# A new order of work on TensorE, with the other engines' queues rearranged to match, in a kernel of two small transformers around a retention layer

## The chip, the cores and the metric

One core of one Trainium2 chip runs the whole program. The metric is the device time of one execution in microseconds (us), median of three runs. TensorE (PE, with its weight loads PEld), VectorE (DVE), ScalarE (ACT) and GpSimd (POOL) each work through a queue of their own in the order in which it is written; semaphores are all that ties them together.

## The reference, cut to what matters

```python
for i in range(6):                                    # DEPTH; x is (1, 2048, 128), run twice: before and after
    x = attn_layer(shift_tokens(x), ...) + x          # a retention layer
    x = ffn_layer(shift_tokens(x), ...) + x
# attn_layer: 16 heads of 64, window 32
q, k, v = x @ Wqkv
q, k = l2norm(q) * qs, l2norm(k) * ksc                # then rotated by tables
sim = q @ k_of_two_windows * 8;  attn = softmax(masked sim);  out = (attn @ v) @ Wo
# ffn_layer
xn = layernorm(x) * g + b;  a, gate = (xn @ W1 + b1);  out = a * gelu(gate) @ W2 + b2
```

All of it is float32. The kernel folds Wv and Wo of a layer into one matrix per head (V'), so that attention's last product, P times V', is summed over the heads in PSUM and gives the layer's output at once.

## The kernel before

The tokens are cut into 16 tiles of 128 per layer, 96 tiles per stack of six layers, and there are two stacks (`stack(0)`, the retention layer, `stack(1)`). A stack is a software pipeline of slots: in slot c each engine runs its part `slot(c, None, s)` with tile n = c at stage 0, tile n-1 at stage 1 and so on to stage 5. The functions are:

- Stage 0: `project_qk(0..3)`, four 128x512 projections of q and k into the two banks of QA, on PE (L838). ACT squares each (`square`, L451), DVE rotates it (`rotate`, L603 and L608) and sums the squares (`square_sum`, L616), POOL adds the two halves of the rotation (`rot_add`, L343). A projection into a bank waits until the projection two before has been rotated. The inverse norm is worked out as NRM (DVE L677), LT and RN (ACT L541, L543), LA and RR (DVE `inverse_norm`, L621, L624, L629); POOL multiplies it in (`norm_mult`, L350).
- Stage 1 and 2: `qk_transpose` (PE L926), four pieces 0 to 3 of four transpositions each, copied to QT and KT by ACT (`qk_out`, L465); `mask_scores` and `scores` (PE L936, L952). The maximum MX and the difference Z are DVE's (L687, L691).
- Stage 3: ACT's exponential of Z (L512), DVE's sums SM and reciprocal RC (L667, L671), POOL's `softmax_mult` (L359). `p_transpose(3, 0)` and, one slot later, `p_transpose(4, 1)` transpose P (PE L881), ACT copies it to PT (`p_out`, L477).
- Stage 4: `project_v(0..3)`, V' in four pieces, 128x32 tiles of the array side by side (PE L902), copied by ACT (`v_out`, L471). Pieces 0 and 1 wait for Z of the previous slot, since they use the banks of the scores; pieces 2 and 3 wait for the copies of 0 and 1.
- Stage 5: `attend`, P times V', 64 matmul instructions of 128x32 (PE L857); ACT copies the result ON (L499); `out_transpose` (PE L865); DVE's `attn_residual` (L635) adds it to Y. In the kernel before DVE does this last part near the end of the slot ahead of PE's `out_transpose`, so it waits there for PE's next slot.

TB has two banks: bank 0 holds P's transpositions and pieces 0 and 3 of q and k, bank 1 holds `attend`, `out_transpose` and pieces 1 and 2. So `qk_transpose(1, 1)` waits for the residual (`s_res`) of tile n-5.

The feed-forward part runs for groups of four tiles. Slots therefore come in fours: the centre slot (c % 4 = 0: `ffn_centre` L965, `ffn_variance` L970, in stack 0 also `fold_weights` L1005), the up0 slot (`ffn_up(.., 0)`, L980 and L981), the up1 slot and the up2 slot (`ffn_up(.., 2)` right behind `project_qk(0)`, and three `ffn_down`, L989). In the last three ACT runs a Gelu (L485) with one table load ahead of it and one behind; DVE's `hidden` (HB, L642) needs it.

PE's order of a slot before, with the feed-forward parts left out, is: `project_qk(0)`, `attend`, `p_transpose(4, 1)`, `project_v(0, 1)`, `out_transpose`, `project_qk(1)`, `qk_transpose(1, 0)` and `(1, 1)`, `project_v(2, 3)`, `project_qk(2, 3)`, `qk_transpose(2, 3)`, `mask_scores`, `qk_transpose(1, 2)`, `scores`, `p_transpose(3, 0)`.

Of the kernel before, what the change touches and what calls it, by code (L numbers as in the profile page):

```python
# [54 lines left out]
def build_macaron(nc, x, w_qk, w_vt, w_out, q_rows, w1, w2, prm_ffn, w_ret, gn, tables, consts, mask_n, ident,  # L55
# [5 lines left out]
    with ctx:  # L61
# [52 lines left out]
        LNB = sb("LNB", [P, 1])  # L114
        RST = sb("RST", [P, 24])
# [204 lines left out]
        def _(po):  # L320
# [5 lines left out]
            po.memset(LNB[:, :], 8.0 * 0.6931471805599453).then_inc(s_cst, 1)  # L326

            def slot(c, it, s):
# [44 lines left out]
                if live(c, 1, it):  # L373
                    norm_mult(1, 1)
                if live(c, 0, it):
                    rot_add(0)
                if live(c, 1, it):
                    norm_mult(1, 2)
                if live(c, 0, it):
                    rot_add(1)  # L380
                if live(c, 3, it):
                    softmax_mult()
                if live(c, 2, it) and (c - 2) % 4 == 3:
                    last_keys()
                if live(c, 0, it):
                    rot_add(2)
                if live(c, 1, it):
                    norm_mult(1, 3)
# [54 lines left out]
        def _(ac):  # L443
            def slot(c, it, s):
# [46 lines left out]
                if up0_g is not None:  # L491
                    ac.wait_ge(s_var, by_group(1, s * GROUPS + up0_g, it, 1))
                    nc.scalar.activation(RS[:, :], FB[:, 1, :], ACT.Ln, bias=EPS[:, 0:1]).then_inc(s_fl, 1)
                    ac.wait_ge(s_fl, by_group(1, s * GROUPS + up0_g, it, 1))
                    nc.scalar.activation(RS[:, :], RS[:, :], ACT.Exp, scale=-0.5).then_inc(s_frs, 1)
                if live(c, 5, it):
                    m = n - 5
                    ac.wait_ge(s_o, by_tile(1, m, it, 1))
                    nc.scalar.activation(ON[:, m % 2, :], TB[:, 1, 0:P], ACT.Copy).then_inc(s_oe, 1)  # L499
                if live(c, 4, it):  # L500
                    p_out(4, 1)
                    v_out(0)
                if live(c, 0, it):
                    square(0)
                if live(c, 4, it):
                    v_out(1)
                if live(c, 0, it):
                    square(1)
                if live(c, 3, it):
                    m = n - 3  # L510
                    ac.wait_ge(s_z, by_tile(1, m, it, 1))
                    nc.scalar.activation(Z[:, m % 2, :], Z[:, m % 2, :], ACT.Exp, scale=8.0).then_inc(s_ex, 1)  # L512
                if live(c, 1, it):
                    qk_out(1, 0)
                    qk_out(1, 1)
                if live(c, 4, it):
                    v_out(2)
                if live(c, 0, it):
                    square(2)
                if live(c, 4, it):  # L520
                    v_out(3)
                if live(c, 0, it):
                    square(3)
# [13 lines left out]
                if live(c, 3, it):  # L537
                    p_out(3, 0)
                if live(c, 0, it):
                    ac.wait_ge(s_rm, by_tile(1, n, it, 1))  # L540
                    nc.scalar.activation(LT[:, n % 2, :], NRM[:, n % 2, :], ACT.Ln, scale=LN_SCALE).then_inc(s_rl, 1)  # L541
                    ac.wait_ge(s_rl, by_tile(1, n, it, 1))
                    nc.scalar.activation(RN[:, n % 2, :], LT[:, n % 2, :], ACT.Exp, scale=-0.5, bias=LNB[:, 0:1])\  # L543
                        .then_inc(s_re, 1)
                if (c - 7) % TPL == 0 and (it is not None or c < TILES):
# [10 lines left out]
            ac.wait_ge(s_cst, 5)  # L556
# [34 lines left out]
        def _(ve):  # L591
            def slot(c, it, s):
# [39 lines left out]
                def attn_residual(rows, one):  # L632
                    m = n - 4
                    a = (m % TPL) * P + one
                    return nc.vector.tensor_tensor(Y2[rows, a:a + P], TB[rows, 1, 0:P], Y[rows, a:a + P], ALU.add)  # L635
# [12 lines left out]
                if live(c, 0, it):  # L648
                    rotate(0)
                    rotate(1)  # L650
                if fold_piece(c, s):
# [8 lines left out]
                if live(c, 0, it):  # L660
                    square_sum(0)
                    square_sum(1)
                if live(c, 3, it):
                    m = n - 3
                    ve.wait_ge(s_ex, by_tile(1, m, it, 1))
                    for e in range(2):
                        nc.vector.tensor_reduce(SM[:, m % 2, e, :], Z[:, m % 2, e * GT:(e + 1) * GT].rearrange(  # L667
                            "p (a c k) -> p c a k", a=2, c=CH), AX.XY, ALU.add).then_inc(s_sum, 1)
                    ve.wait_ge(s_sum, by_tile(2, m, it, 2))
                    need(ve, s_pn, by_tile(2, m - 1, it))  # L670
                    nc.vector.reciprocal(RC[:, m % 2, :, :], SM[:, m % 2, :, :]).then_inc(s_rc, 1)  # L671
                if live(c, 0, it):
# [23 lines left out]
                if live(c, 0, it):  # L696
                    inverse_norm()
# [21 lines left out]
                if live(c, 4, it):  # L719
# [21 lines left out]
            ve.wait_ge(s_cst, 5)  # L741
# [81 lines left out]
        def _(pe):  # L823
            mm = nc.tensor.matmul

            def slot(c, it, s):
# [195 lines left out]
                if up2_g is not None:  # L1022
                    ffn_up(up2_g, 2)
                if live(c, 5, it):
# [9 lines left out]
                if live(c, 0, it):  # L1034
                    project_qk(1)
                if live(c, 1, it):
                    qk_transpose(1, 0)
                    qk_transpose(1, 1)
                if live(c, 4, it):
                    project_v(2)  # L1040
                    project_v(3)
                if live(c, 0, it):
# [208 lines left out]
```

## Time and profile before

| | |
|---|---|
| median of 3 runs | 3528.91 us (3528.77 to 3534.39) |
| the profiled execution, its time / its span | 3533.1 us / 3531.3 us |
| busy share PE, DVE, ACT, POOL | 96%, 81%, 67%, 66% |
| mean granted TensorE clock | 0.984 |
| four slots in the middle of stack 1 | 66.58 us, PE busy throughout |

The profile shows one execution. A row of the timeline is a run of instructions of one line: its start in us from the span's start, its length, and in brackets how long the engine was idle before and what ended that. Matmuls are pipelined and a matmul's length includes its drain, so what a block costs on PE is the distance from its start to the next block's start.

### The profile page before, as it was taken

The page shows a single profiled execution, that of the slowest core. Times are in us where ns is not written, and L with a number is a line of the kernel's source. Part 1 is how long each engine was busy: PE and PEld are TensorE (multiplying, and loading weights), DVE is VectorE, ACT ScalarE, POOL GpSimd, SP SyncE. Part 2 cuts the span into 40 slices and gives each one's busy share as a digit, 9 for nine tenths or more (in the row PEclk, how much of TensorE's full clock was granted, in tenths as well). Part 3 has the DMA queues.
Part 4 walks back from the last instruction along what each step waited for, and adds up shares of the span by engine and source line. Part 5 has one row for each costly group of instructions (what it writes and reads, how often), then busy time and mean ns, then how long its engine had stood idle before and what let it go on. Part 6 is the DMA issues. An engine that isn't in the chain of part 4 may idle for free.

```text
span 3531.3 us, 123143 instructions
## 1 busy us (share of the span) xinstructions
PE 3402.0 (96%) x51660; PEld 1851.7 (52%) x51660; DVE 2847.4 (81%) x6052; ACT 2365.6 (67%) x4133; POOL 2333.9 (66%) x2187
## 2 busy tenths in 40 slices
PE   6999999999999999999788999999999999999996
PEld 3555555555555555555354555555555555555553
DVE  6888888888888888886468888888888888888883
ACT  3676677667677667767424777677767767767764
POOL 5766667676677677775137777677677677667761
PEclk8999999999999999999998999999999999999998
DMA  2001001001001001000100000000000000000000
GB/s 83 11 14 47 12 14 47 13 15 47 12 14 47 13 14 35 9 12 20 38 2 23 14 23 22 17 23 22 12 29 22 12 27 23 12 27 10 12 5 13
DMA packets 49223, 76.64 MB, mean 22 GB/s; under 512 B 7072, under 2 KB 37024, under 8 KB 47136
## 3 DMA queue, kind: packets, MB, share of 16 engines
q1 hardware_dynamic: 48672, 68.76, 6.1%
q8 instruction: 411, 6.73, 0.8%
q14 instruction: 140, 1.15, 0.1%
HBM read 61.39 MB, written 7.34 MB: 19 GB/s over the span
## 4 chain that ended last, share of the span: by engine, by line
PE 93%; DVE 3%; issue 2%; POOL 1%; ACT 1%; DMA 0%; SPq 0%; DVEq 0%; POOLq 0%; ACTq 0%
PE VS L902 20%; PE QA L838 19%; PE TB L857 10%; PE TB L926 9%; PE VS L952 8%; PE TB L881 6%; PE FB L980 4%; PE FB L989 4%; PE FB L981 4%; PE VS L936 2%; PE TB L865 1%; PE FB L965 1%; PE FB L970 1%; DVE T L608 1%; POOL QN L343 0%
## 5 line engine op out<-in xcount | busy, mean ns | idle before, releaser
L343 POOL TENSOR_TENSOR QN<-T 128x512 f32<-128x512 f32 x768 | 979.9, 1276 | 578.6 <-DVE T L608 578.6
L350 POOL TENSOR_TENSOR QN<-QN,RR 128x512 f32<-128x512 f32 x768 | 800.7, 1043 | 296.9 <-DVE RR L629 296.9
L838 PE MATMUL QA<-WQ,Y 128*128 128x512 f32 x1536 | 797.8, 618 | 20.2 <-DVE T L608 12.1
L902 PE MATMUL VS<-MW,Y 128*32 128x512 f32 x6144 | 741.8, 600 | 5.0 <-DVE Z L691 5.0
L451 ACT ACTIVATE SQ<-QA 128x512 f32<-128x512 f32 x768 | 458.8, 597 | 294.0 <-PE QA L838 268.7
L608 DVE TENSOR_TENSOR T<-QA,TAB 128x256 f32<-128x256 f32 x1536 | 570.7, 412 | 0.0
L603 DVE TENSOR_TENSOR T<-QA,TAB 128x512 f32<-128x512 f32 x768 | 513.6, 669 | 38.1 <-ACT SQ L451 23.2
L471 ACT ACTIVATE V<-VS 128x512 f32<-128x512 f32 x768 | 461.0, 600 | 95.1 <-PE VS L902 94.5
L926 PEld LDWEIGHTS TB<-CST,QN 128*128 128x128 f32 x3072 | 374.2, 142 | 256.8 <-issue 191.6
L359 POOL TENSOR_TENSOR Z<-Z,RC 128x512 f32<-128x512 f32 x384 | 394.5, 1048 | 142.8 <-DVE RC L671 142.8
L616 DVE TENSOR_REDUCE SSQ<-SQ 128x8 f32<-128x512 f32 x768 | 487.2, 676 | 0.0
L635 DVE TENSOR_TENSOR Y<-TB,Y 64x128 f32<-64x128 f32 x384 | 111.2, 290 | 464.6 <-PE TB L865 461.9
L926 PE MATMUL TB<-CST,QN 128*128 128x128 f32 x3072 | 437.9, 275 | 15.0 <-POOL QN L350 14.3
L838 PEld LDWEIGHTS QA<-WQ,Y 128*128 128x128 f32 x1536 | 263.1, 199 | 309.5 <-DVE T L608 176.3
L857 PEld LDWEIGHTS TB<-V,PT 128*32 128x32 f32 x12288 | 325.9, 110 | 153.1 <-issue 111.8
L857 PE MATMUL TB<-V,PT 128*32 128x128 f32 x12288 | 381.5, 274 | 4.4 <-issue 4.3
L477 ACT ACTIVATE PT<-TB 128x512 f32<-128x512 f32 x384 | 228.9, 596 | 196.5 <-PE TB L881 196.2
L902 PEld LDWEIGHTS VS<-MW,Y 128*32 128x32 f32 x6144 | 161.0, 109 | 300.3 <-issue 295.0
L952 PEld LDWEIGHTS VS<-KT,QT 64*32 64x32 f32 x24576 | 255.7, 105 | 105.0 <-issue 88.2
L465 ACT ACTIVATE KT<-TB 128x512 f32<-128x512 f32 x384 | 231.6, 603 | 116.2 <-PE TB L926 116.2
L952 PE MATMUL VS<-KT,QT 64*32 64x64 f32 x24576 | 290.8, 225 | 16.0 <-issue 15.9
L687 DVE TENSOR_REDUCE MX<-VS 128x8 f32<-128x512 f32 x384 | 245.4, 679 | 29.9 <-PE VS L952 25.7
(166 smaller groups left out, 4206.0 us busy)
## 6 DMA issues: line engine op xcount, KB each, us to landing
TAB<-in_tables SPq DMA_DIRECT2D x192, 128.0 KB, 2.1
WQ<-in_w_qk SPq DMA_DIRECT2D x48, 256.0 KB, 2.9
m_dram<-MW SPq DMA_DIRECT2D x6, 1024.0 KB, 5.4
MW<-m_dram SPq DMA_DIRECT2D x6, 1024.0 KB, 5.2
W1R<-in_w SPq DMA_DIRECT2D x12, 341.0 KB, 3.0
WS<-in_w_vt SPq DMA_DIRECT2D x6, 512.0 KB, 5.9
WS<-in_w_out SPq DMA_DIRECT2D x6, 512.0 KB, 7.8
W<-in_w SPq DMA_DIRECT2D x12, 192.0 KB, 2.4
```

Source lines behind the costliest of these rows:

```text
L343: po.tensor_tensor(QN[:, n % 2, k, :], T1[:, k, :], T2[:, k, :], ALU.add).then_inc(s_add, 1)
L350: po.tensor_tensor(heads(QN[:, m % 2, k, :]), heads(QN[:, m % 2, k, :]), RR[:, m % 2, 8 * k:8 * k + 8].unsqueeze(2).to_broadcast([P, 8, DH ...
L451: nc.scalar.activation(SQ[:, k % 2, :], QA[:, k % 2, :], ACT.Square).then_inc(s_sq, 1)
L471: nc.scalar.activation(V4[:, m % 4, w, :], VS[:, w % 2, :], ACT.Copy).then_inc(s_ve, 1)
L603: nc.vector.tensor_tensor(heads(T1[:, k, :]), heads(QA[:, b, :]), tab[:, 0:DHEAD].unsqueeze(1).to_broadcast([P, 8, DHEAD]), ALU.mult)
L608: ins = nc.vector.tensor_tensor(t2[:, :, half, :], q2[:, :, 1 - half, :], tab[:, DHEAD + 32 * half:DHEAD + 32 * half + 32].unsqueeze(1).to ...
L616: nc.vector.tensor_reduce(SSQ[:, n % 2, 8 * k:8 * k + 8], heads(SQ[:, k % 2, :]), AX.X, ALU.add)\
L838: mm(QA[:, k % 2, :], Y[:, j * P:(j + 1) * P], WQ[:, k, :], start=True, stop=True).then_inc(s_qk, 1)
L857: last = mm(TB[32 * w:32 * w + 32, 1, 0:P], PT[:, m % 2, b, 32 * w:32 * w + 32], v, start=(b == 0), stop=(b == CH - 1), tile_position=(0, ...
L902: last = mm(VS[32 * q:32 * q + 32, w % 2, :], Y[:, a:a + WIN], MW[:, l % 2, q, :], start=True, stop=True, tile_position=(0, 32 * q), skip_ ...
L926: last = nc.tensor.transpose(TB[:, (0, 1, 1, 0)[k], b * P:(b + 1) * P], QN[:, m % 2, k, b * P:(b + 1) * P], IDF)
L952: last = mm(bank[32 * w:32 * w + 32, :, ch, :], QT[r, m % 2, ch, w * WIN:(w + 1) * WIN], KT[r, ch, a:a + 2 * WIN].rearrange("p (a k) -> p ...
```

## The change

The order within a slot is rewritten on four engines; the instructions stay the same but one. PE: `project_qk(1)` moves up behind `project_qk(0)`, `p_transpose(4, 1)` stands ahead of `attend`, `attend` stands directly ahead of `project_v(0, 1)`, and the three blocks `qk_transpose(1, 0)`, `out_transpose`, `qk_transpose(1, 1)` stand in different places: the first two behind `project_v(0, 1)`, the last behind `project_v(2, 3)`. DVE: `attn_residual` now handles tile n-5 behind the first two square sums, the fold copy is later, `inverse_norm` stands ahead of MX and Z instead of behind them, and NRM is a TENSOR_TENSOR maximum with a constant tile TINY instead of a TENSOR_SCALAR. ACT: squares 0 and 1, `p_out(4, 1)` and the exponential come first, LT and RN stand ahead of `p_out(3, 0)`. POOL: `norm_mult(1, 2)` and `(1, 3)` come one and two places earlier.

```diff
 PE
                 if live(c, 0, it):
                     project_qk(0)
                 if up2_g is not None:
                     ffn_up(up2_g, 2)
+                if live(c, 0, it):
+                    project_qk(1)
+                if live(c, 4, it):
+                    p_transpose(4, 1)
                 if live(c, 5, it):
                     attend()
                 if live(c, 4, it):
-                    p_transpose(4, 1)
                     project_v(0)
                     project_v(1)
+                if live(c, 1, it):
+                    qk_transpose(1, 0)
                 if live(c, 5, it):
                     out_transpose()
                 if fold_piece(c, s):
                     fold_weights(*fold_piece(c, s))
-                if live(c, 0, it):
-                    project_qk(1)
-                if live(c, 1, it):
-                    qk_transpose(1, 0)
-                    qk_transpose(1, 1)
                 if live(c, 4, it):
                     project_v(2)
                     project_v(3)
+                if live(c, 1, it):
+                    qk_transpose(1, 1)
                 if live(c, 0, it):
                     project_qk(2)
 DVE
                 if live(c, 0, it):
                     rotate(0)
                     rotate(1)
+                    square_sum(0)
+                    square_sum(1)
+                if live(c, 5, it):
+                    ve.wait_ge(s_ot, by_tile(1, n - 5, it, 1))
+                    attn_residual(*HALVES[0])
+                    attn_residual(*HALVES[1]).then_inc(s_res, 1)
...
-                    nc.vector.tensor_scalar_max(NRM[:, n % 2, :], SSQ[:, n % 2, :], 1e-24).then_inc(s_rm, 1)
+                    nc.vector.tensor_tensor(NRM[:, n % 2, :], SSQ[:, n % 2, :], TINY[:, :], ALU.max).then_inc(s_rm, 1)
                 if up1_g is not None:
                     hidden(up1_g, 1)
                 if live(c, 0, it):
                     rotate(3)
+                    inverse_norm()
                 if live(c, 2, it):
...
-                if live(c, 0, it):
-                    inverse_norm()
...
-                if live(c, 4, it):
-                    ve.wait_ge(s_ot, by_tile(1, n - 4, it, 1))
-                    attn_residual(*HALVES[0])
-                    attn_residual(*HALVES[1]).then_inc(s_res, 1)
                 if up0_g is not None:
                     hidden(up0_g, 0)
 ACT, new order
+                square(0), square(1), p_out(4, 1), exponential(3), ON copy(5), v_out(0), v_out(1), qk_out(1, 0),
+                v_out(2), v_out(3), qk_out(1, 1), square(2), square(3), qk_out(2, 3)
...
                 if live(c, 1, it):
                     qk_out(1, 2)
-                if live(c, 3, it):
-                    p_out(3, 0)
                 if live(c, 0, it):
                     (LT, RN)
+                if live(c, 3, it):
+                    p_out(3, 0)
```

## Rows read from the trace of the kernel before

**Rows 1.** The page, busy time and share of the span.
```profile
PE 3402.0 (96%) x51660; PEld 1851.7 (52%) x51660; DVE 2847.4 (81%) x6052; ACT 2365.6 (67%) x4133; POOL 2333.9 (66%) x2187
```

**Rows 2.** Windows: four slots of stack 1; length, busy times, granted clock.
```profile
2899.40:2966.00 66.60, 66.60 (x1061) 36.09 (x1060) 56.72 (x124) 47.96 (x84) 47.78 (x45) 1.00 0.03 10
```

**Rows 3.** Timeline of PE, the up1 slot from 2931.41 us on.
```profile
2931.41 1.02 PE L838 MATMUL QA<-WQ,Y 128*128 128x512 f32 x2
2932.36 1.95 PE L857 MATMUL TB<-V,PT 128*32 128x128 f32 x64
2934.24 0.66 PE L881 MATMUL TB<-CST,Z 128*128 128x128 f32 x4
2934.83 1.92 PE L902 MATMUL VS<-MW,Y 128*32 128x512 f32 x16
2936.68 0.33 PE L865 MATMUL TB<-CST,ON 128*128 128x128 f32 x1
2936.85 1.02 PE L838 MATMUL QA<-WQ,Y 128*128 128x512 f32 x2
2937.71 1.04 PE L926 MATMUL TB<-CST,QN 128*128 128x128 f32 x8
2938.68 1.92 PE L902 MATMUL VS<-MW,Y 128*32 128x512 f32 x16
2940.53 1.98 PE L838 MATMUL QA<-WQ,Y 128*128 128x512 f32 x4
2942.35 0.60 PE L926 MATMUL TB<-CST,QN 128*128 128x128 f32 x4
...
2947.43 1.02 PE L838 MATMUL QA<-WQ,Y 128*128 128x512 f32 x2
```

**Rows 4.** Groups by line: busy us, mean ns of one, idle before.
```profile
L857 PEld LDWEIGHTS TB<-V,PT 128*32 128x32 f32 x12288 | 325.9, 110 | 153.1 <-issue 111.8
...
L704 DVE SCALAR_TENSOR_TENSOR Y<-FB,PRB,Y 64x512 f32<-64x512 f32 x96 | 71.8, 748 | 13.1 <-PE FB L989 12.4
```

**Rows 5.** Timeline of DVE, end of the up0 slot and the up1 slot.
```profile
2931.02 1.29 DVE L687 TENSOR_REDUCE MX<-VS 128x8 f32<-128x512 f32 x2
...
2933.42 0.18 DVE L621 TENSOR_TENSOR LA<-RN 128x32 f32<-128x32 f32 x1
...
2933.86 0.19 DVE L629 SCALAR_TENSOR_TENSOR RR<-LA,RN 128x32 f32<-128x32 f32 x1
2937.05 0.59 DVE L635 TENSOR_TENSOR Y<-TB,Y 64x128 f32<-64x128 f32 x2 [2.99 <-PE TB L865]
2937.67 0.75 DVE L642 SCALAR_TENSOR_TENSOR HB<-FB,PRB,GE 128x512 f32<-128x512 f32 x1
2938.34 0.68 DVE L603 TENSOR_TENSOR T<-QA,TAB 128x512 f32<-128x512 f32 x1
...
2940.86 1.27 DVE L616 TENSOR_REDUCE SSQ<-SQ 128x8 f32<-128x512 f32 x2
2942.05 1.27 DVE L667 TENSOR_REDUCE SM<-Z 128x8 f32<-128x512 f32 x2
```

**Rows 6.** Timeline of ACT, end of the up0 slot and the up1 slot.
```profile
2929.60 0.69 ACT L485 ACTIVATE GE<-FB,PRB 128x512 f32<-128x512 f32 x1 [0.57 <-PE FB L981]
2930.31 1.28 ACT L531 ACT_TABLE_LOAD   x1
2931.61 0.60 ACT L465 ACTIVATE QT<-TB 128x512 f32<-128x512 f32 x1
2932.10 0.59 ACT L477 ACTIVATE PT<-TB 128x512 f32<-128x512 f32 x1
2932.58 0.23 ACT L541 ACTIVATE LT<-NRM 128x32 f32<-128x32 f32 x1
2932.84 0.32 ACT L543 ACTIVATE RN<-LT,LNB 128x32 f32<-128x32 f32 x1
...
2938.41 1.05 ACT L512 ACTIVATE Z<-Z 128x1024 f32<-128x1024 f32 x1
```

More of the change, by code:

```diff
@@ L114, in build_macaron @@
         LNB = sb("LNB", [P, 1])
+        TINY = sb("TINY", [P, 32])
         RST = sb("RST", [P, 24])
@@ L326, in _ @@
             po.memset(LNB[:, :], 8.0 * 0.6931471805599453).then_inc(s_cst, 1)
+            po.memset(TINY[:, :], 1e-24).then_inc(s_cst, 1)
             def slot(c, it, s):
@@ L374, in slot @@
                     norm_mult(1, 1)
+                    norm_mult(1, 2)
                 if live(c, 0, it):
@@ L377, in slot @@
                 if live(c, 1, it):
-                    norm_mult(1, 2)
+                    norm_mult(1, 3)
                 if live(c, 0, it):
@@ L495, in slot @@
                     nc.scalar.activation(RS[:, :], RS[:, :], ACT.Exp, scale=-0.5).then_inc(s_frs, 1)
+                if live(c, 0, it):
+                    square(0)
+                    square(1)
+                if live(c, 4, it):
+                    p_out(4, 1)
+                if live(c, 3, it):
+                    m = n - 3
+                    ac.wait_ge(s_z, by_tile(1, m, it, 1))
+                    nc.scalar.activation(Z[:, m % 2, :], Z[:, m % 2, :], ACT.Exp, scale=8.0).then_inc(s_ex, 1)
                 if live(c, 5, it):
@@ L500, in slot @@
                 if live(c, 4, it):
-                    p_out(4, 1)
                     v_out(0)
-                if live(c, 0, it):
-                    square(0)
-                if live(c, 4, it):
                     v_out(1)
-                if live(c, 0, it):
-                    square(1)
-                if live(c, 3, it):
-                    m = n - 3
-                    ac.wait_ge(s_z, by_tile(1, m, it, 1))
-                    nc.scalar.activation(Z[:, m % 2, :], Z[:, m % 2, :], ACT.Exp, scale=8.0).then_inc(s_ex, 1)
                 if live(c, 1, it):
                     qk_out(1, 0)
-                    qk_out(1, 1)
                 if live(c, 4, it):
                     v_out(2)
+                    v_out(3)
+                if live(c, 1, it):
+                    qk_out(1, 1)
                 if live(c, 0, it):
                     square(2)
-                if live(c, 4, it):
-                    v_out(3)
-                if live(c, 0, it):
                     square(3)
@@ L544, in slot @@
                         .then_inc(s_re, 1)
+                if live(c, 3, it):
+                    p_out(3, 0)
                 if (c - 7) % TPL == 0 and (it is not None or c < TILES):
@@ L650, in slot @@
                     rotate(1)
+                    square_sum(0)
[4 more added lines that the diff above has]
+                    attn_residual(*HALVES[1]).then_inc(s_res, 1)
+                if live(c, 3, it):
+                    m = n - 3
+                    ve.wait_ge(s_ex, by_tile(1, m, it, 1))
+                    for e in range(2):
+                        nc.vector.tensor_reduce(SM[:, m % 2, e, :], Z[:, m % 2, e * GT:(e + 1) * GT].rearrange(
+                            "p (a c k) -> p c a k", a=2, c=CH), AX.XY, ALU.add).then_inc(s_sum, 1)
+                    ve.wait_ge(s_sum, by_tile(2, m, it, 2))
+                    need(ve, s_pn, by_tile(2, m - 1, it))
+                    nc.vector.reciprocal(RC[:, m % 2, :, :], SM[:, m % 2, :, :]).then_inc(s_rc, 1)
                 if fold_piece(c, s):
@@ L660, in slot @@
                 if live(c, 0, it):
[L661 to L672, printed above, removed]
                     rotate(2)
@@ L739, in pads @@
                 nc.vector.memset(Y2[64:128, 0:1], 0.0)
-            ve.wait_ge(s_cst, 5)
+            ve.wait_ge(s_cst, 6)
             pads()
@@ L1023, in slot @@
                     ffn_up(up2_g, 2)
+                if live(c, 0, it):
+                    project_qk(1)
+                if live(c, 4, it):
+                    p_transpose(4, 1)
                 if live(c, 5, it):
@@ L1041, in slot @@
                     project_v(3)
+                if live(c, 1, it):
+                    qk_transpose(1, 1)
                 if live(c, 0, it):
```

12 lines of the change are left out of this document (3 added, 9 removed).

## The prediction

> **What bounds the kernel now.** The page comes first: PE is busy 96% of the span, DVE 81%, ACT and POOL two thirds [rows 1]. Then the windows, to see whether that share means the same in the steady part: over four slots of stack 1 PE is busy 66.60 of 66.60 us at the full clock, while DVE has 10 us to spare and ACT and POOL 19 each [rows 2]. So nobody keeps PE waiting there, and a slot is as long as the sum of PE's blocks. The timeline of PE tells what a block costs, as the distance between starts [rows 3]; DVE's and ACT's timelines tell how late their parts of a slot are [rows 5, 6]. The reader should note DVE's wait of 2.99 us ahead of the residual: DVE, which must do the residual for the slot to come, stands still until PE has got to `out_transpose` [rows 5]. It does no harm today, because PE asks for what lies behind it later still.
>
> **What PE's order costs.** Within one kind of work the price is flat. A projection is 0.86 (2936.85 to 2937.71). A transposition is 0.11: eight of them and a change to the 128x32 form take 0.97, four and such a change 0.59. Changes of form cost extra [rows 3]:
> - full to 128x32: 0.95 from the projection to `attend`, less 0.86, is 0.09;
> - 128x32 back to full: a pair of V' pieces takes 1.85 where four times 0.43 is 1.72, so 0.13 (this holds a little for the first group of the block too);
> - the first full instruction behind it is slow as well: a lone transposition takes 0.17 instead of 0.11, so 0.06; two projections there take 1.82 instead of 1.72, so 0.10.
>
> Before, a slot has four excursions into tiled forms: `attend`, the two pairs of V', the scores. After, `attend` and the first pair are one. That saves 0.09 + 0.13 + 0.06 = 0.28. Behind the second pair there now stands a transposition in place of a projection: 0.10 becomes 0.06, a saving of 0.04 to 0.05. Splitting `qk_transpose(1, 0)` from `(1, 1)` costs nothing more, since each borders on an excursion that is there anyway. Sum 0.33 a slot. About 188 of the 192 tiles have all these neighbours (the first and last slots of a stack do not), so 188 x 0.33 = 62 us.
>
> Here the join itself was never run: the trace has no 128x32 block behind another. If its weight loads did not hide, 0.13 would stay; if they hide as inside `attend`, nothing does. Inside `attend` 12288 loads of 110 ns, 1352 us laid end to end, take 325.9 us of busy time, so four are under way at once, all of them on 128 rows, while the matmuls run on [rows 4]. I take nothing for the join and keep 0.13 x 188 = 24 us as the other bound.
> The Trainium skill speaks against the change here: "TensorE: Matmul & The Clock Gate", section "Part 3: Packing small matmuls", says that a weight load overlaps with matmuls in flight only when its row group differs, and all of these share theirs. By that rule the join would be exposed and the saving 0.20 a slot, 38 us, by my rows' prices. The L857 row does not look like it.
>
> **What must now be on time.** New starts on PE, counted from `project_qk(0)`, in a slot without feed-forward work ahead: `project_qk(1)` 0.86, `p_transpose(4, 1)` 1.72, `attend` 2.25 (four transpositions 0.44, change 0.09), `project_v(0)` 4.00 (1.88 less the 0.13 of the change back), `qk_transpose(1, 0)` 5.85, `out_transpose` 6.34, `project_v(2)` 6.55, `qk_transpose(1, 1)` 8.40, `project_qk(2)` 8.89. All distances are those of [rows 3].
>
> The weak point is DVE's new order. `inverse_norm` now stands ahead of MX and Z and waits for RN. In an up0 or up1 slot RN is late, because on ACT it stands behind the Gelu, a table load and the QT copy. The up0 slot's chain, from the start of its Gelu, is:
> - ACT: Gelu to table load 0.71, table load 1.30, QT 0.49 to the next, LT 0.26, RN 0.32: 3.08 [rows 6];
> - DVE: from LA to RR 0.44, and 0.11 to the next: 0.55; MX and Z 2.40; `hidden` 0.67; two rotations 2.52; two square sums 1.19; the residual 0.59: 7.92 [rows 5];
> - two hand-overs between engines at 0.04 each, as `out_transpose` ends at 2937.01 and the residual starts at 2937.05 [rows 3, 5]: 0.08.
>
> That is 11.08 us, and only then may `qk_transpose(1, 1)` of the up1 slot write TB's second bank, which the residual reads. The Gelu starts 1.81 before the slot's end (2929.60 against 2931.41), and nothing ahead of it changes. So the transposition can start 9.27 into the up1 slot, and PE is there at 8.40: a stall of 0.87. Behind it on PE are `project_qk(2)`, `(3)` and the rest of the slot, all of which slip. Two smaller waits fall inside it: `p_out(3, 0)`, now behind RN, ends at 1.9 where PE asks at 1.72, and Z ends at 4.3 where `project_v(0)` asks at 4.00 plus the first slip.
> It happens wherever the slot after an up0 slot has a live tile, 22 times a stack: 44 x 0.87 = 38 us.
>
> In the up2 slot PE has 1.72 more ahead of the same transposition and the residual is on time (10.2 against 10.3). But ACT has two table loads and the third Gelu ahead of squares, `p_out(4, 1)`, exponential, ON and V copies. From the Gelu of the up1 slot: 3.08 to RN's end; p_out 0.61, load 1.30, Gelu 0.70, load 1.30, then square, square, p_out at 0.49 each, exponential 0.95 (1.05 long, 0.1 overlapped as in its neighbours), ON 0.19, V 0.60: 10.2 [rows 6]. Less 1.81, V' piece 0 is copied at 8.4, and `project_v(2)`, which overwrites that bank, is due at 6.55 + 1.72 = 8.27. Stall 0.15, some 46 times: 7 us.
>
> The other slots stay free. Centre slot: in the up2 slot before it no table load stands ahead of RN, Z ends 2.3 into it, then come the two halves of Y's write at 0.7 [rows 4], two rotations, two square sums and the residual as above, done at 8.0 against 8.40; up0 slot: DVE starts at 2.5 and waits for `out_transpose`, residual done at 7.3. `project_qk(1)`, now early, needs rotation 3 of the slot before, which ends a microsecond or more ahead of the slot's end, or, where `hidden` pushes it past the end, has the up2 block of 1.72 in front. NRM as TENSOR_TENSOR saves DVE some tenths, in time in which it then waits for RN: nothing. POOL's moves are hidden: its inputs come from DVE, and it has 19 us in 66.6 free [rows 2]. TINY is one memset at the start. No DMA moves. The fold copy in stack 0 (centre slot) has the 0.8 us that PE spends on folding as cover.
>
> **Sum.** -62 + 38 + 7 = -17 us against the profiled execution's 3533.1 us, which is 3516. That execution lay 4.2 above the median, so the median should be 3512.
>
> **Rivals.**
> - *PE keeps all it saves.* The chain would have to be 0.9 us shorter, so that no new wait is seen: 3528.9 - 62 = 3467. DVE's 10 free us in 66.6 and the 2.99 us wait that goes away speak for it [rows 2, 5]; the order `RN, then MX and Z` against it, which moves the free time to a worse place. Chance 0.07.
> - *The join is exposed.* 0.13 stays in every slot: 3512 + 24, less what the shorter saving takes off the waits (PE arrives 0.13 later, so 90 times up to 0.13, some 12): 3524, within 0.2% of before. Together with other ways to come out level: chance 0.14. The skill's rule above would give this; the L857 row is against it.
> - *Slower: ACT in the up2 slot.* The copies behind its last table load are priced at 0.49 from start to start [rows 6]. If, in the new neighbourhood, each waits for its predecessor's 0.60, the seven of them on that chain add 0.8: 46 x 0.8 = 37 us, and the median would be 3549. Net zero is reached at 0.37 per up2 slot. Against it: QT to PT 0.49 in the same place. With other waits of this size that I do not see (a chain over three engines has many edges), chance 0.15.
>
> **How the numbers follow.** The forecast, a part of the saving kept, has 0.64; it runs from 3495 (stall 0.5 instead of 0.87) to 3522. A measurement of this kernel tells 0.2%, 7 us, from no change. Faster: 0.64 + 0.07, with a little of the forecast's upper end given to level: 0.69. Same 0.15, slower 0.16. The range is 3490 to 3534: it leaves out the full saving (0.07) and most of the slower case (0.13).
>
> **What would show it.** In the after profile: slots of four 66.58 - 4 x 0.33 + 1.0 = 66.2 us. `attend` to `project_v(0)` 1.77 apart; V' pair to `qk_transpose(1, 0)` 1.83 to 1.85. In up1 slots PE idle ahead of the L926 block behind the second V' pair, released by DVE's residual, some 0.9; in up2 slots a gap ahead of `project_v(2)`, released by ACT's V copy. On DVE an idle of 2.4 us ahead of LA in up0 slots, released by ACT's RN, and none of 2.99 ahead of the residual. The prediction is wrong if LA does not wait in up0 slots, if the join costs, or if another wait on PE shows in centre or up0 slots.

## The result, and the profile after

The changed kernel takes 3483.5 us (median of 4 runs, 3483.0 to 3490.1), the kernel before 3529.9 beside it: ratio 0.9871, 95% interval 0.9853 to 0.9888, 46 us faster. The forecast was 3512 with a range from 3490 to 3534; the direction was right and the size far too small. The profiled execution has a span of 3481.8 us, 49.5 less than before.

The page after, busy time of the engines and the groups with the pauses (busy us, mean ns | idle before, releaser), first of the kernel after:

```profile
PE 3337.9 (96%) x51660; PEld 1871.0 (54%) x51660; DVE 2858.4 (82%) x6052; ACT 2433.7 (70%) x4133; POOL 2342.3 (67%) x2188
...
L854 PE MATMUL TB<-V,PT 128*32 128x128 f32 x12288 | 375.2, 274 | 0.0
...
L949 PE MATMUL VS<-KT,QT 64*32 64x64 f32 x24576 | 289.0, 225 | 8.5 <-issue 8.1
```

and the same two groups of the kernel before, `attend` (L857) and `scores` (L952), as the page has them:

```profile
L857 PE MATMUL TB<-V,PT 128*32 128x128 f32 x12288 | 381.5, 274 | 4.4 <-issue 4.3
...
L952 PE MATMUL VS<-KT,QT 64*32 64x64 f32 x24576 | 290.8, 225 | 16.0 <-issue 15.9
```

PE is still 96% busy, of a shorter span: 64 us of its own busy time have gone, with the same 51660 matmul instructions. An idle "issue" is one for which the page names no releaser; it has gone inside `attend` and halved inside `scores`. No term of the forecast had that.

The timeline of PE after, up1 slot from 2425.80 us on, the counterpart of [rows 3] (L835 projections, L878 P's transpositions, L854 `attend`, L899 V', L862 `out_transpose`, L923 transpositions of q and k):

```profile
2425.80 1.88 PE L835 MATMUL QA<-WQ,Y 128*128 128x512 f32 x4
2427.70 0.63 PE L878 MATMUL TB<-CST,Z 128*128 128x128 f32 x4
2428.26 1.96 PE L854 MATMUL TB<-V,PT 128*32 128x128 f32 x64
2430.20 1.92 PE L899 MATMUL VS<-MW,Y 128*32 128x512 f32 x16
2432.06 0.66 PE L923 MATMUL TB<-CST,QN 128*128 128x128 f32 x4
2432.55 0.27 PE L862 MATMUL TB<-CST,ON 128*128 128x128 f32 x1
2432.75 1.92 PE L899 MATMUL VS<-MW,Y 128*32 128x512 f32 x16
2435.16 0.63 PE L923 MATMUL TB<-CST,QN 128*128 128x128 f32 x4 [0.48 <-DVE Y L634]
2435.62 1.88 PE L835 MATMUL QA<-WQ,Y 128*128 128x512 f32 x4
...
2442.36 0.59 PE L835 MATMUL QA<-WQ,Y 128*128 128x512 f32 x1
```

This slot is 16.56 long; before it was 16.02. The second pair of V' pieces starts at 2432.75, and the transposition behind it 2.41 later where 1.85 is the price: it waits for DVE's residual, as forecast. (The idle of 0.48 in brackets is counted from the end of the drain, so the distance of starts shows more of the loss.) The two other losses are 0.18 ahead of `p_transpose(4, 1)`, which starts 1.90 after the projections instead of 1.72, and 0.17 between `attend` and V'.

DVE and ACT of the same stretch, as in [rows 5, 6]:

```profile
2424.03 0.75 DVE L607 TENSOR_TENSOR T<-QA,TAB 128x256 f32<-128x256 f32 x2
2427.11 0.19 DVE L620 TENSOR_TENSOR LA<-RN 128x32 f32<-128x32 f32 x1 [2.32 <-ACT RN L540]
...
2427.67 1.28 DVE L690 TENSOR_REDUCE MX<-VS 128x8 f32<-128x512 f32 x2
2428.87 1.28 DVE L694 TENSOR_TENSOR Z<-VS,MX 128x512 f32<-128x512 f32 x2
2430.06 0.74 DVE L641 SCALAR_TENSOR_TENSOR HB<-FB,PRB,GE 128x512 f32<-128x512 f32 x1
2430.72 0.68 DVE L602 TENSOR_TENSOR T<-QA,TAB 128x512 f32<-128x512 f32 x1
...
2434.43 0.58 DVE L634 TENSOR_TENSOR Y<-TB,Y 64x128 f32<-64x128 f32 x2
```

```profile
2424.00 0.69 ACT L486 ACTIVATE GE<-FB,PRB 128x512 f32<-128x512 f32 x1 [0.64 <-PE FB L978]
2424.71 1.28 ACT L530 ACT_TABLE_LOAD   x1
2426.00 0.60 ACT L466 ACTIVATE QT<-TB 128x512 f32<-128x512 f32 x1
2426.50 0.22 ACT L538 ACTIVATE LT<-NRM 128x32 f32<-128x32 f32 x1
2426.75 0.32 ACT L540 ACTIVATE RN<-LT,LNB 128x32 f32<-128x32 f32 x1
```

DVE is idle for 2.32 us ahead of LA, in the middle of a slot, for ACT's RN; from the Gelu at 2424.00 to the residual's end at 2435.01 it is 11.01 us, and the forecast's chain had 11.08. The wait of 2.99 us ahead of the residual [rows 5] is gone.

**Where the 49.5 us of the span come from.** The usual length of each kind of slot (the distance from one `project_qk(0)` to the next, median over the slots of that kind), both traces:

| slot | before | after | times | in all |
|---|---|---|---|---|
| centre | 15.97 | 15.64 | 25 | -8 |
| centre with fold | 16.81 | 16.28 | 19 | -10 |
| up0 | 16.03 | 15.64 | 44 | -17 |
| up1 | 16.03 | 16.56 | 44 | +23 |
| up2, without / with the `ffn_bias` block | 18.55 / 19.70 | 18.25 / 19.40 | 32 / 10 | -13 |
| sum | | | | -25 |

The other 24.5 are not in the usual slots. Summed over the places inside `attend` and `scores` where the next matmul starts over 0.2 or 0.15 us after the last, behind the first 120 us, TensorE paused 40 times for 25.9 us before (15 in `attend`, 6.0 us; 25 in `scores`, 19.9 us) and 15 times for 11.5 us after, all in `scores`: -14.4. (The page's idle "issue" is smaller, since it is counted from the modelled end of the matmul before.) Of the last 10, some 5 lie in the other slots of the two stacks, from the ninth on: outside `attend` and `scores` they run over their usual length by 6.5 us in all before and by 1.7 after. The other 5.5 lie at the ends: the first eight slots of the two stacks give 3.5, what follows the start of the very last slot gives 3.8, and the start and the stretch around the retention layer take back 1.8.

### The profile page after: what moved, and what is told of

It is laid out like the page before. It is cut to its first block, busy times and chain, and to the rows that moved or that the text cites. A ratio compares the mean times of both kernels' runs of the same rounds, so it can differ in the third digit from the quotient of the medians.

```text
span 3481.8 us, 123144 instructions
## 1 busy us (share of the span) xinstructions
PE 3337.9 (96%) x51660; PEld 1871.0 (54%) x51660; DVE 2858.4 (82%) x6052; ACT 2433.7 (70%) x4133; POOL 2342.3 (67%) x2188
## 4 chain that ended last, share of the span: by engine, by line
PE 51%; POOL 22%; issue 15%; DVE 10%; ACT 1%; POOLq 0%; DMA 0%; SPq 0%; DVEq 0%; ACTq 0%
PE QA L835 10%; PE VS L899 10%; POOL QN L345 8%; POOL QN L352 8%; PE TB L923 6%; PE TB L854 5%; PE VS L949 4%; PE FB L986 4%; POOL Z L361 3%; PE TB L878 3%; DVE T L607 3%; DVE T L602 3%; PE FB L977 3%; PE FB L978 2%; POOL TAB L337 2%
## 5 line engine op out<-in xcount | busy, mean ns | idle before, releaser
L352 POOL TENSOR_TENSOR QN<-QN,RR 128x512 f32<-128x512 f32 x768 | 792.6, 1042 | 154.4 <-DVE RR L628 154.4
L835 PE MATMUL QA<-WQ,Y 128*128 128x512 f32 x1536 | 753.5, 603 | 23.0 <-DVE T L607 14.7
L899 PE MATMUL VS<-MW,Y 128*32 128x512 f32 x6144 | 738.5, 598 | 6.7 <-DVE Z L694 6.4
L602 DVE TENSOR_TENSOR T<-QA,TAB 128x512 f32<-128x512 f32 x768 | 525.4, 684 | 187.1 <-ACT SQ L452 178.2
L923 PEld LDWEIGHTS TB<-CST,QN 128*128 128x128 f32 x3072 | 354.3, 141 | 491.8 <-issue 278.1
L452 ACT ACTIVATE SQ<-QA 128x512 f32<-128x512 f32 x768 | 441.4, 595 | 193.6 <-PE QA L835 182.2
L923 PE MATMUL TB<-CST,QN 128*128 128x128 f32 x3072 | 483.9, 280 | 34.4 <-DVE Y L634 20.9
L835 PEld LDWEIGHTS QA<-WQ,Y 128*128 128x128 f32 x1536 | 268.1, 193 | 245.9 <-issue 208.5
L854 PE MATMUL TB<-V,PT 128*32 128x128 f32 x12288 | 375.2, 274 | 0.0
L854 PEld LDWEIGHTS TB<-V,PT 128*32 128x32 f32 x12288 | 323.6, 110 | 33.4 <-issue 33.3
L899 PEld LDWEIGHTS VS<-MW,Y 128*32 128x32 f32 x6144 | 172.8, 109 | 282.3 <-issue 243.2
L505 ACT ACTIVATE Z<-Z 128x1024 f32<-128x1024 f32 x192 | 203.9, 1062 | 66.9 <-DVE Z L694 65.9
```

Of the source, the lines that this page charges most:

```text
L352: po.tensor_tensor(heads(QN[:, m % 2, k, :]), heads(QN[:, m % 2, k, :]), RR[:, m % 2, 8 * k:8 * k + 8].unsqueeze(2).to_broadcast([P, 8, DH ...
L602: nc.vector.tensor_tensor(heads(T1[:, k, :]), heads(QA[:, b, :]), tab[:, 0:DHEAD].unsqueeze(1).to_broadcast([P, 8, DHEAD]), ALU.mult)
L835: mm(QA[:, k % 2, :], Y[:, j * P:(j + 1) * P], WQ[:, k, :], start=True, stop=True).then_inc(s_qk, 1)
L854: last = mm(TB[32 * w:32 * w + 32, 1, 0:P], PT[:, m % 2, b, 32 * w:32 * w + 32], v, start=(b == 0), stop=(b == CH - 1), tile_position=(0, ...
L899: last = mm(VS[32 * q:32 * q + 32, w % 2, :], Y[:, a:a + WIN], MW[:, l % 2, q, :], start=True, stop=True, tile_position=(0, 32 * q), skip_ ...
L923: last = nc.tensor.transpose(TB[:, (0, 1, 1, 0)[k], b * P:(b + 1) * P], QN[:, m % 2, k, b * P:(b + 1) * P], IDF)
```

## The experiments

Each is compared with the kernel before, run on the same chip beside it; the changed kernel stands at 0.9871.

**1. The inverse norm behind MX and Z again**, the changed kernel otherwise.

```diff
                     rotate(3)
-                    inverse_norm()
...
                     ins.then_inc(s_z, 1)
+                if live(c, 0, it):
+                    inverse_norm()
```

> The changed kernel with one part undone: on VectorE the inverse norm stands behind MX and Z again. Chain theory (the up1 slot loses 0.92 us because MX and Z wait behind an inverse norm that waits for ScalarE's RN): the MX of an up0 slot starts 0.4 us before the slot's end instead of 1.8 us into the next, the residual of the up1 slot is done at about 7.6 us against a transposition due at 8.40, and of the 0.92 us only the 0.18 us ahead of p_transpose(4, 1) stay, since p_out(3, 0) still stands behind RN. 44 x 0.74 = 33 us less than the changed kernel, about 3451 us. Rival (the wait comes from the residual's new place as such, behind two rotations and two square sums): the gap ahead of the second transposition stays, at most 10 us gained.

Measured: 3491.1 us, ratio 0.9877 (0.9863 to 0.9892), not faster than the changed kernel. The wait for RN is gone and the up1 slot is 16.21 us instead of 16.56, but the centre slot is 16.21 instead of 15.64. The chain theory's half that said which wait goes was right; what it said of the time was wrong, because another wait, of 0.62 us in the centre slot and 0.42 in the up1 slot, came ahead of the same transposition. The timeline of the centre slot that starts at 2399.41 shows where it comes from, all engines together:

```profile
2401.87 0.19 DVE L628 SCALAR_TENSOR_TENSOR RR<-LA,RN 128x32 f32<-128x32 f32 x1
2401.98 1.51 DVE L706 SCALAR_TENSOR_TENSOR Y<-FB,PRB,Y 64x512 f32<-64x512 f32 x2
2402.14 1.05 POOL L352 TENSOR_TENSOR QN<-QN,RR 128x512 f32<-128x512 f32 x1 [3.27 <-DVE RR L628]
...
2403.14 0.73 POOL L337 TENSOR_TENSOR TAB<-TAB,QROW 128x256 f32<-128x256 f32 x1
...
2403.96 0.69 DVE L602 TENSOR_TENSOR T<-QA,TAB 128x512 f32<-128x512 f32 x1 [0.48 <-issue]
```

RR is late, so POOL's `norm_mult(0, 0)` is late, and in its queue the rotation's table (L337) stands behind it; DVE's `rotate(0)` starts 0.09 us after the table's end. So the inverse norm early buys the table early, and late it costs on POOL what it gives on DVE.

**2. As 1, and `p_out(3, 0)` ahead of LT and RN.**

```diff
                 if live(c, 1, it):
                     qk_out(1, 2)
+                if live(c, 3, it):
+                    p_out(3, 0)
```

> As the run before, and on ScalarE p_out(3, 0) stands ahead of LT and RN again. Chain theory: the last 0.18 us of the up1 slot go as well, 44 x 0.18 = 8 us, about 3443 us, and all slots are as long as the sum of TensorE's blocks (15.64, 15.64, 15.64, 18.21 us). Rival: RN, now 0.5 us later, delays the inverse norm and VectorE passes that on, so no gain over the run before, or a loss.

Measured: 3496.2 us, ratio 0.9893 (0.9876 to 0.9909). The 0.18 us ahead of `p_transpose(4, 1)` did go, and came back in full behind V' (0.62 instead of 0.42), so the up1 slot stays at 16.21. The wait that ends last was still the one behind the table. The rival was right on the time, for another reason than it gave: the inverse norm was not delayed, RR starts 2.46 us into the up1 slot in both runs.

**3. `attend` and the first pair of V' products parted again.**

```diff
-                if live(c, 4, it):
-                    p_transpose(4, 1)
                 if live(c, 5, it):
                     attend()
                 if live(c, 4, it):
+                    p_transpose(4, 1)
                     project_v(0)
```

> The changed kernel with P times V' and the first pair of V' products parted again: p_transpose(4, 1) stands between them. Form theory (each excursion of TensorE into a tiled form costs 0.09 in, 0.13 out and 0.06 on the first instruction behind it): 0.28 us more in every slot except where a wait takes it up anyway, which is the up1 slot; about 144 x 0.28 = 40 us more than the changed kernel, about 3524 us. Rival (the saving came from the other moves and from fewer pauses for instructions): under 15 us more.

Measured: 3519.4 us (9 runs), ratio 0.9970 (0.9958 to 0.9981), 36 us more than the changed kernel against 40 expected. Slots (centre, up0, up1, up2) are 15.92, 15.92, 16.56 and 18.50 us: 0.28, 0.28, 0 and 0.25 more. The price of an excursion is shown, and so is that the up1 slot takes it up inside its wait.

**4. The kernel before with `project_qk(1)` alone moved up.**

```diff
                 if up2_g is not None:
                     ffn_up(up2_g, 2)
+                if live(c, 0, it):
+                    project_qk(1)
                 if live(c, 5, it):
                     attend()
...
-                if live(c, 0, it):
-                    project_qk(1)
                 if live(c, 1, it):
                     qk_transpose(1, 0)
```

> The kernel before with one part of the change alone: project_qk(1) stands behind project_qk(0), all other queues as before. TensorE's blocks cost the same in this order, so by the form theory the time stays. Instruction theory (TensorE pauses inside attend and scores when it has used up its instructions faster than they are fetched, 39 pauses and 26 us in the kernel before, 15 and 12 us after, those in attend all gone because attend stands 1.3 us further from the scores): attend stands 0.86 us later here, its 13 pauses (about 6 us) get fewer, time 3 to 8 us less, 3522 to 3527 us. Rival (the pauses fall by chance of where the fetched blocks end): as many pauses in attend as before, time within 2 us of before.

Measured: 3627.1 us, ratio 1.0266 (1.0251 to 1.0281), 94 us slower. Neither theory had that. PE's timeline, from an up2 slot:

```profile
2407.22 0.33 PE L865 MATMUL TB<-CST,ON 128*128 128x128 f32 x1
2407.39 0.60 PE L926 MATMUL TB<-CST,QN 128*128 128x128 f32 x4
2408.32 0.63 PE L926 MATMUL TB<-CST,QN 128*128 128x128 f32 x4 [0.34 <-DVE Y L635]
```

In the kernel before, `project_qk(1)` between `out_transpose` and the transpositions gave the residual its 0.86 us. Without it `qk_transpose(1, 1)` stands 0.93 behind `(1, 0)` where 0.44 is the price. Centre, up0 and up2 slots are 0.53 us longer than before and up1 slots 0.80, since `mask_scores` waits there too, 0.27 longer; the centre slots with a fold, where the fold still stands behind `out_transpose`, lose nothing. That makes the 94 us. I had costed the move at nothing without naming what it covered. The pauses inside `attend` fell from 15 to 3 (1.1 us), as the instruction theory said.

**5. As 1, and the table of the next tile ahead of `rot_add(3)`.**

```diff
-                if live(c, 0, it):
-                    table()
+                if c == 0:
+                    table(0)
...
+                if c + 1 < TILES:
+                    table(c + 1)
                 if live(c, 0, it):
                     rot_add(3)
                     norm_mult(0, 0)
```

> The first experiment again (inverse norm behind MX and Z), and on GpSimd the table of the next tile is multiplied ahead of rot_add(3) and norm_mult(0, 0) instead of at the next slot's start. Table theory (in the first experiment the waits of 0.62 us in the centre slot and 0.42 us in the up1 slot came because rotate(0) waits for the table, the table stands behind norm_mult(0, 0) in GpSimd's queue, and that waits for the inverse norm): both waits go, only the 0.18 us ahead of p_transpose(4, 1) in the up1 slot stay; slots of 15.64, 15.64, 15.82 and 18.22 us, 0.74 us per four slots less than the changed kernel, about 3483.5 - 33 = 3450 us. Rival (VectorE has simply too much to do in these slots): the waits ahead of the second transposition stay within 0.1 us and the time is that of the first experiment, 3491 us.

Measured: 3439.8 us, ratio 0.9745 (0.9730 to 0.9759). Slots 15.77, 15.64, 15.84 and 18.24 us: the waits behind V' are gone but for 0.13 in many centre slots. It is 10 us better than expected; the first eight slots of the two stacks are shorter too (207.6 us together, 222.1 in the changed kernel).

**6. As 5, and `p_out(3, 0)` ahead of LT and RN.**

> As the run before, with p_out(3, 0) ahead of LT and RN on ScalarE. Table theory: no wait is left in any of the four kinds of slot, 8 us less than the run before, about 3443 us. Rival: RN 0.5 us later delays the inverse norm, or TensorE's pauses for instructions grow as its other waits go (15.3 us of them in the second experiment against 11.5 in the changed kernel), and the gain over the run before is nil.

Measured: 3434.7 us (3427.0 to 3436.6), ratio 0.9727 (0.9711 to 0.9742): 96 us under the kernel before and 49 under the changed one, the fastest here. The up1 slot, from one block of four projections (L838) to the next:

```profile
2455.47 1.88 PE L838 MATMUL QA<-WQ,Y 128*128 128x512 f32 x4
2457.18 0.60 PE L881 MATMUL TB<-CST,Z 128*128 128x128 f32 x4
2457.72 1.96 PE L857 MATMUL TB<-V,PT 128*32 128x128 f32 x64
2459.49 1.90 PE L902 MATMUL VS<-MW,Y 128*32 128x512 f32 x16
...
2462.01 1.92 PE L902 MATMUL VS<-MW,Y 128*32 128x512 f32 x16
2463.87 0.66 PE L926 MATMUL TB<-CST,QN 128*128 128x128 f32 x4
```

Every distance is the price of the block: 1.71, 0.54, 1.77, and 1.86 from V' to the transposition where the changed kernel has 2.41. That all waits go was not quite right: the usual centre slot without a fold keeps 0.12 (15.76). The step over experiment 5 is 5 us, 8 were expected; the intervals of the two overlap.

**7. The changed kernel with the early table alone.**

> The changed kernel with the early table alone. In the changed kernel the inverse norm is done early in the centre and up2 slots, and in the up1 slot rotate(0) is behind MX, Z and a Gelu product that wait for RN, not behind the table (done at 3.8 us into the slot, rotation due at 4.9). Table theory: no change, 3481 to 3486 us. Rival (the table is a bound in the changed kernel too): the up1 slot gets shorter than 16.56 us.

Measured: 3477.3 us, ratio 0.9849 (0.9832 to 0.9865), overlapping the changed kernel's interval. All kinds of slot keep their lengths (15.64, 15.64, 16.56, 18.25), so the table bounds nothing in the usual slots. The few microseconds by which it is lower have two places in the trace: the pauses in `scores` are 8.1 us instead of 11.5, and the first eight slots of the two stacks take 218.9 us instead of 222.1.

**8. The three blocks of transpositions together:** `qk_transpose(1, 1)` directly behind `out_transpose`.

```diff
                 if live(c, 5, it):
                     out_transpose()
+                if live(c, 1, it):
+                    qk_transpose(1, 1)
```

> The changed kernel with qk_transpose(1, 1) directly behind out_transpose, ahead of the second pair of V' products. Residual theory (that piece may not start before VectorE's residual has read TB's second bank, and the residual itself stands behind two rotations and two square sums): it is due at 6.45 us into a slot, 8.2 in the up2 slot, and the residual is done at 8.0, 7.3, 9.3 and 10.1 us in the four kinds; stalls of 1.6, 0.9, 2.8 and 1.9 us, some of it given back since VectorE then has time to catch up: 150 to 300 us more than the changed kernel. Rival (the piece's place costs and gains nothing but the price of forms): within 10 us of it.

Measured in a single run: 3922.5 us, 439 more than the changed kernel, well beyond what was expected. The timeline of PE and, below it, windows over that wait, the stretch behind it and the next (length, busy times, then the granted clock):

```profile
2427.16 0.27 PE L862 MATMUL TB<-CST,ON 128*128 128x128 f32 x1
2429.77 1.09 PE L923 MATMUL TB<-CST,QN 128*128 128x128 f32 x4 [2.34 <-DVE Y L634]
2430.79 1.08 PE L899 MATMUL VS<-MW,Y 128*32 128x512 f32 x4
```

```profile
2424.80:2429.70 4.90, 2.63 (x25) 0.94 (x21) 4.86 (x12) 2.90 (x5) 4.33 (x5) 0.98 0.00 0
2429.70:2433.00 3.30, 3.23 (x16) 1.31 (x20) 1.49 (x3) 0.21 (x1) 2.25 (x3) 0.51 0.01 2
2433.00:2440.00 7.00, 7.00 (x154) 3.81 (x146) 3.29 (x7) 5.64 (x9) 1.63 (x2) 1.00 0.02 4
```

The residual's wait is there (2.34 us), and behind it TensorE runs at the lower of its two levels, 1.2 GHz, for this window of 3.3 us: four transpositions take 1.02 instead of 0.53. The same wait stands in all 44 up1 slots from the ninth slot of a stack on. In 37 of them the clock fell, and such a slot usually takes 20.24 us; in the other 7 it did not, and the slot takes 18.61. So a fall costs 1.6 us here and does not always follow. There are 61 falls in these slots of all kinds, some 100 of the 439 us. Over the run the granted clock is 0.960 against 0.985. So a long wait can be paid for twice, which my estimate left out. That the piece must stand behind the second V' pair in this order is shown.

**9. The changed kernel with `attend` back behind `project_qk(0)`.**

```diff
+                if live(c, 5, it):
+                    attend()
                 if live(c, 0, it):
                     project_qk(1)
                 if live(c, 4, it):
                     p_transpose(4, 1)
-                if live(c, 5, it):
-                    attend()
```

> The changed kernel with attend moved back to directly behind project_qk(0), where it stood before; all else stays. It starts 0.95 us into the slot instead of 2.25, as before, and is again an excursion of its own (0.28 us a slot, seen in the third experiment). Instruction theory (attend pauses when it follows the scores too closely): 10 to 15 pauses and 4 to 6 us of them inside attend come back, the time is that of the third experiment plus that, about 3523 us. Rival (which blocks of instructions end where decides, not the distance): attend has 0 to 3 pauses, as in the third experiment (2 pauses, 1.4 us), and the time is 3519 us.

Measured: 3541.2 us (10 runs), ratio 1.0024 (1.0014 to 1.0034), slower than expected by 18 us. This one move takes back all that the change gained, and a little more: 58 us by the medians, 54 by the ratios. The pauses inside `attend` came back, 16 of them and 8.1 us. One, with the start of the second part of the block:

```profile
2364.28 1.73 PE L854 MATMUL TB<-V,PT 128*32 128x128 f32 x53 [0.81 <-issue]
```

The usual slots are 0.045 us longer than in experiment 3, since it is now a projection that stands behind the tiled form (0.10 instead of 0.06). Between the profiled executions of the two experiments lie 17 us (22 between the medians): some 6.5 are that, 6.7 the pauses inside `attend`, and 3.3 those inside `scores` (15.7 against 12.4), in which nothing was moved.

**10. Half of the score products left out.** The kernel issues two of the four windows' products in `scores`, so its output is not the reference's.

```diff
-                            for w in range(4):
+                            for w in range(0, 4, 2):
```

> The changed kernel with half of the score products left out: only 64 of the 128 matmul instructions (two of four windows) are issued in scores, the other windows keep the mask alone. The block takes 0.7 instead of 1.41 us, 192 x 0.7 = 135 us less of TensorE's work if nothing else becomes the bound. Instruction theory: with 256 fewer instructions of 518 gone from the slot's densest 1.4 us, the pauses inside scores (15, 11.5 us in the changed kernel) go to 0 to 3. Rival (the pauses are waits for something else that scores meets): as many as before.

(64 matmul instructions fewer are, with their weight loads, 128 entries fewer a slot, not the 256 of the expectation.)

Measured in a single run: 3443.5 us. No pause over 0.15 us is left in `scores` or 0.2 in `attend`. The time fell by 40 us only, not 135. Half of the products don't take half of the block: it is 1.03 us from its start to the next (2441.82 to 2442.85) instead of 1.41, so 0.38 and not 0.7 is saved, and up1 and up2 slots stay at 16.55 and 18.25, set by the waits for DVE and ACT. So the block is both shorter and thinner here, and the run alone can't say which of the two ends the pauses.

```profile
2441.82 1.10 PE L949 MATMUL VS<-KT,QT 64*32 64x64 f32 x64
2442.85 0.65 PE L878 MATMUL TB<-CST,Z 128*128 128x128 f32 x4
```

**The pauses, over the runs.** Distance of `attend` from the slot's start in a slot without up2 work, and pauses inside it: 0.95 us, 15 pauses, 6.0 us (before) and 16, 8.1 us (experiment 9); 1.81 us, 2 pauses, 1.4 us (experiment 3) and 3, 1.1 us (experiment 4); 2.25 us, none (after, experiments 1, 2, 5, 6, 7). `scores` ends 0.5 us ahead of the slot's start. `scores` and `attend` together are 384 of some 518 weight loads and matmuls of a slot and take 3.3 of its 16 us. That the pauses come from instructions used up faster than they arrive fits all of it: they go where two such blocks stand apart, and where one is halved.

The traces go further. The page lists the transfers of the instruction queue; here is its row before and in experiment 10:

```profile
q8 instruction: 411, 6.73, 0.8%
```

```profile
q8 instruction: 315, 5.16, 0.6%
```

Each transfer brings 16384 bytes. Count all that the trace has on TensorE (weight loads, matmuls and what its sequencer does) in order of start, and cut the count at every 256, with the first cut behind 193 entries, the same in all runs: that gives 411 cuts before and after and 315 in experiment 10, as many as there are transfers. Every pause found here, 41 before and 16 after (with the one of each in the first 120 us) and all those of experiments 1 to 9, ends exactly at such a cut, and 1.2 to 1.6 us after the end of a transfer. None stands anywhere else in the two blocks. So what TensorE waits for in these pauses is its next 256 instructions. The shortest piece takes 1.41 us in the traces of before and after and 5.15 in experiment 10, which has no pauses. Before, 96 cuts fall inside `attend` and 15 of them are pauses; after, 97 and none. That `attend` pauses less further from `scores` is shown by experiment 9. Why `scores` itself, in which nothing was moved and into which 192 cuts fall in both, has 25 pauses before and 10 to 19 in the other runs stays open: two traces of one kernel were not compared, so how far it varies by itself isn't known.

## Why the prediction was wrong, step by step

- **Forms of the tiled blocks: right.** Saving forecast 0.33 us a slot; centre and up0 slots give 0.33 and 0.39, experiment 3 gives 0.28 for the excursion alone. The join hides its weight loads: `attend` to V' is 1.77 us in experiment 6, and was 1.88 to the full form [rows 3]. The Trainium skill ("TensorE: Matmul & The Clock Gate", "Part 3: Packing small matmuls") lets a weight load overlap with matmuls in flight only when its row group differs. These loads share theirs, and the trace does not agree: 16 groups of four, 0.11 us apart, make up the 1.77 us, and nothing is left for the join.
- **The up1 slot's wait: right in mechanism, place and size.** 0.87 forecast; 16.56 less 15.64 is 0.92, with DVE's residual as releaser and the idle of 2.32 ahead of LA (2.4 forecast). Experiments 1, 5 and 6 remove it.
- **The up2 slot's wait: mis-sized.** 0.15 forecast, 0.04 measured (18.25 against 18.21 where nothing waits), half of it ahead of `project_v(2)` and half ahead of the transposition behind the second pair. After RN's start ACT starts `p_out(3, 0)` 0.23 later (2443.31 to 2443.54), not 0.32, and ON takes 0.15 to the next instead of 0.19. That is 5 of the missing microseconds. (The steps from `p_out` to V in that sum stand in the trace, but not in [rows 6], which it names.)
- **Fold slots and the mask: left out.** "The fold copy in stack 0 has the 0.8 us that PE spends on folding as cover" looked at DVE alone. On PE the fold is itself a tiled block; behind it there now stands another tiled block instead of a projection, which saves 0.20 more (0.53 against 0.33), 4 us. In up0 and up1 slots `mask_scores` no longer waits 0.05 us: `qk_transpose(2, 3)` to the mask was 0.48 (from 2942.35 in [rows 3] to 2942.83) and is 0.44. The mask waits for the copy of V' piece 3, which ACT now does ahead of square 2. In experiment 4, where this wait is longer, the trace names ACT's V copy as what ended it; in the kernel before it is too short to be listed. Another 4 us.
- **The sum: the step that failed.** "-62 + 38 + 7 = -17" treated all 3533.1 us as the sum of blocks and waits for semaphores. With the two points above the usual slots give -25. But PE also lost 26 us in pauses inside `attend` and `scores`, in which it waited for its instructions, and the sum has no term for them: 14.4 us of them went. Of these the 6.0 inside `attend` went because it moved from 0.95 to 2.25 us behind the slot's start (experiment 9 brings them back); why 8.4 went inside `scores` is open. The waits table of before shows them as idle "issue". Some 5 us more went in other slots of the stacks that ran over their usual length, and 5.5 at the ends of the stacks, which I had priced at nothing. No single one of these would have put the forecast right.
- **NRM: mis-sized, without a known effect.** "Some tenths" was the saving of the TENSOR_TENSOR form. The TENSOR_SCALAR took 0.98 us in the median before (0.18 at the least), the new form takes 0.19. In up0 and up1 slots DVE then waits for RN, as forecast; no run has this part of the change alone, so what it gave elsewhere is not shown.
- **What would show it.** All the signs named came: slots of four of 66.09 us (66.2 forecast), `attend` to V' 1.77, the waits in up1 and up2 slots and none in the usual centre and up0 slots. They tested the usual slots and could not see what lay outside the sum.
- **The range** reached down to 3490. It was built from the bounds of the terms that I had, with the full saving (3467, chance 0.07) left out; a term that is missing has no bound.
- **Rivals.** The changed kernel does not keep all that it saves: the rival at 3467 is off by 16 us and its mechanism (no new wait) is false. The exposed join and ACT's slower copies did not happen.

## What to carry to other kernels

When the bound engine is full, first write down what each block costs next to each of its neighbours, from starts, and count idle "issue" inside dense blocks as a term of its own: it moves when dense blocks move. Then follow each edited queue to the next engine: an operation that moves ahead of others brings its own wait with it, and one that moves back delays all that stands behind its consumer in the consumer's queue. A block that seems free to move may be what hides a wait (experiment 4, 94 us); and the two halves of a repair may be worth nothing until both are made (experiment 1 is level with the changed kernel by their ratios, 0.9877 and 0.9871; experiment 5 is 44 us faster).

## What the runs showed of the hardware

- TensorE can fall short of instructions: pauses of 0.1 to 2.2 us inside blocks of 128 and 256 small instructions, 26 us in the kernel before and none when half of the score products are left out. All end at a multiple of 256 instructions, 1.2 to 1.6 us after the end of a transfer of 16384 bytes on the instruction queue.
- In experiment 8 a wait of 2.34 us on TensorE was followed by 3.3 us at 1.2 GHz (granted clock 0.51). Of 44 such waits 37 had a fall of the clock behind them, at 1.6 us each. The waits and pauses of up to 0.56 us idle in four slots of the changed kernel (2461.76 to 2528.63 us) left its window at 1.00.
- A change from 128x32 tiles to the full array costs 0.13 us and another 0.06 on a transposition or 0.10 on a projection behind it; two 128x32 blocks of different shapes back to back cost nothing at the join.
